# Attention loop on one Trainium2 core: the product with V issued for two loop steps together, at every second step

## What is computed

```python
qkv = x @ qkv_w.T + qkv_b
q, k, v = jnp.split(qkv, 3, axis=2)
scores = jnp.einsum('hbds,hbdt->hbst', q, k) / jnp.sqrt(jnp.float32(hd))
w = jax.nn.softmax(scores, axis=-1)
attn = jnp.einsum('hbst,hbdt->hbsd', w, v)
return attn @ out_w.T + out_b
```

## Time and profile before

| | |
|---|---|
| median of three runs | 601.78 us |
| the profiled execution | 601.03 us |
| its span, first to last instruction | 599.0 us |
| TensorE matmuls busy | 548.1 us (92%) |
| VectorE busy | 479.6 us (80%) |
| ScalarE busy | 349.2 us (58%) |
| L1257, the product with V | 1024 matmuls, 189.5 to 558 us |

### The profile page before, as it was taken

How to read it: one execution, slowest core, us unless ns; L and a number is a source line. 1 busy time by engine, 2 the same in 40 slices (tenths; PEclk the granted TensorE clock), 3 DMA queues, 4 the chain that set the end, 5 groups by cost and what they waited for, 6 DMA issues and landing times.

```text
span 599.0 us, 9634 instructions
## 1 busy us (share of the span) xinstructions
PE 548.1 (92%) x2831; PEld 218.8 (37%) x2831; DVE 479.6 (80%) x965; ACT 349.2 (58%) x667; POOL 112.2 (19%) x155
## 2 busy tenths in 40 slices
PE   2986899885699999999999998999999999999797
PEld 1442567473112333332333332233323333323366
DVE  6999668984598888988888888688888888853573
ACT  2765223245004677777777776677777777778551
POOL 5955906644000001001001000000000000000000
PEclk9997999898555999999999999899999999999999
DMA  8020000013330112001101100200200000000001
GB/s 202 20 52 20 1 1 2 5 48 97 111 113 2 39 43 69 15 1 51 32 2 35 47 2 18 69 2 2 79 2 2 2 2 2 1 2 1 1 19 54
DMA packets 14903, 18.95 MB, mean 32 GB/s; under 512 B 4040, under 2 KB 13175, under 8 KB 13687
## 3 DMA queue, kind: packets, MB, share of 16 engines
q1 hardware_dynamic: 14058, 17.54, 9.8%
q0 software_dynamic: 240, 0.46, 0.7%
q10 hardware_dynamic: 550, 0.27, 0.2%
HBM read 12.75 MB, written 4.19 MB: 28 GB/s over the span
## 4 chain that ended last, share of the span: by engine, by line
PE 73%; DVE 17%; DMA 3%; ACT 3%; issue 2%; SPq 1%; POOL 0%; ACTq 0%; DVEq 0%
PE ps L1257 21%; PE ps L1230 20%; PE ps L1295 18%; PE ps L1035 6%; PE ps L1045 5%; DVE acc L795 3%; DVE mx L896 3%; DVE h L711 2%; DMA k_scr<-gate 1%; DVE acc L841 1%; PE ps L1244 1%; ACT gate L649 1%; DMA kt<-k_scr 1%; DVE st L688 1%; ACT acc L649 1%
## 5 line engine op out<-in xcount | busy, mean ns | idle before, releaser
L896 DVE TENSOR_REDUCE mx<-ps 128x1 f32<-128x512 f32 x512 | 318.8, 681 | 46.6 <-PE ps L1230 41.3
L649 ACT ACTIVATE gate<-ps 128x512 f32<-128x512 f32 x256 | 134.3, 604 | 87.4 <-PE ps L1295 87.4
L1230 PE MATMUL ps<-kt,qt 72*128 72x512 bf16 x384 | 157.7, 417 | 10.6 <-DMA kt<-k_scr 10.6
L649 ACT ACTIVATE acc<-ps 128x512 f32<-128x512 f32 x256 | 132.1, 602 | 49.6 <-PE ps L1295 49.6
L1295 PE MATMUL ps<-qt,kt 96*128 96x512 bf16 x384 | 143.1, 387 | 3.2 <-issue 2.0
L1230 PEld LDWEIGHTS ps<-kt,qt 72*128 72x128 bf16 x384 | 38.3, 100 | 127.0 <-DVE mx L896 83.4
L1257 PE MATMUL ps<-gate,v 128*32 128x512 f32 x512 | 69.1, 611 | 0.7 <-ACT o_sb L640 0.7
L1257 PE MATMUL ps<-acc,v 128*32 128x512 f32 x512 | 69.0, 612 | 0.6 <-ACT acc L649 0.6
L447 POOL CAST nm_s<-nm 16x128 bf16<-16x128 f32 x16 | 4.6, 284 | 305.6 <-DVE nm L909 305.6
L1295 PEld LDWEIGHTS ps<-qt,kt 96*128 96x128 bf16 x384 | 37.4, 99 | 45.5 <-ACT gate L649 6.7
L1230 PE MATMUL ps<-val 72*128 72x512 bf16 x128 | 48.8, 382 | 0.0
(11 more groups left out here) (181 smaller groups left out, 473.7 us busy)
## 6 DMA issues: line engine op xcount, KB each, us to landing
qt<-q_scr SPq DMA_DIRECT2D x18, 192.0 KB
kt<-k_scr SPq DMA_DIRECT2D x18, 192.0 KB
val<-q_scr SPq DMA_DIRECT2D x6, 192.0 KB
val<-k_scr SPq DMA_DIRECT2D x6, 192.0 KB
x<-in_L_attn_a_x SPq DMA_DIRECT2D x4, 256.0 KB, 4.7
us<-h SPq DMA_DIRECT2D x8, 128.0 KB, 2.4
out<-x SPq DMA_DIRECT2D x4, 256.0 KB, 2.2
q_scr<-attn SPq DMA_DIRECT2D x6, 128.0 KB
```

Of the source, the lines that this page charges most:

```text
L649: act.activation(pexp[s % NPB][:, j, :], bank(exp_bank(n0, s * QH + j, last)[0]), ACT.Exp, scale=SCALE).then_inc(exp_done, 1)
L896: dve.tensor_reduce(mx[:, half, u // 2, u % 2:u % 2 + 1], bank(MBANKS[k % 4]), AX.X, ALU.max).then_inc(m_read, 1)
L1230: pe.matmul(bank(MBANKS[k % 4]), qt[r][0:QK_ROWS, half, j, c * P:(c + 1) * P], kt[r][0:QK_ROWS, keys, j, :], start=True, stop=True).then_i ...
```

## The change

```diff
@@ -1295,9 +1295,11 @@
                             j += 1
-                        elif kind == "v" and s:
+                        elif kind == "v" and s % 2 == 0 and s:
+                            pv(r, n, s - 2)
                             pv(r, n, s - 1)
-                        elif kind == "v" and not first:
+                        elif kind == "v" and s == 0 and not first:
+                            pv(prev, n - 1, STEPS - 2)
                             pv(prev, n - 1, STEPS - 1)
@@ -1328,6 +1330,7 @@
             quad(NQ - 1, 0, False, True)
+            pv((NQ - 1) % NBUF, NQ - 1, STEPS - 2)
             pv((NQ - 1) % NBUF, NQ - 1, STEPS - 1)
```

## The result

The changed kernel takes 592.39 us (median of four runs, 591.92 to 593.38), the kernel before 601.44 (600.37 to 601.83) beside it. The ratio is 0.9854 with a 95% interval of 0.9836 to 0.9873: faster by 1.5%, 9.0 us. The forecast was 593.0. The profiled executions stand 9.1 us apart (601.03 and 591.92 us).

What follows compares the result with a forecast made beforehand. TensorE was taken as the bound; 10.4 us saved by pairs + 0.4 at `copy_o` - 0.5 at `turn_o` - 1.5 in quad 7 = 8.8 us, giving 593.0 us (forecast 591 to 595, range 590.5 to 599).

Steps and rivals of the forecast that it cites:

- The bound: Attention loop: TensorE sets the pace, busy the whole window from 192 to 372 us; half a quad takes 23.34 us.
- The junction: Between two adjacent `pv` on TensorE: the second follows like a `pv`'s own second round, 0.455 us, at most 0.63.
- Rivals 1 and 2: Second `pv`'s weight loads exposed, 0.11 us per junction, 599.9 us (chance 0.08); junction costs full turnaround, 0.18 us, 604.3 (0.09).
- The size of a pair: TensorE, two `pv` together: one change in and one out saved, 0.18 us per pair, 10.4 us over 58 pairs.
- The two small terms: First `pv` of a half no longer behind `copy_o`: 0.4 us gained; eighth "m" late at `turn_o`: 0.5 us lost.
- Quad 7: Last quad, no "m" between the "e" from step 4: each pair 0.3 us longer, 1.5 us lost over five.
- The loop's return: Return of the loop: costs 2.4 us once, put down to issue; left out since nothing lengthens the code.
- The room in the banks: Sixteen bf16 matmuls in a row: banks last, with 0.13, 0.09 and 0.04 us to spare; 0.03 late at `turn_o`.
- ScalarE's room: Eighth "e" behind a pair: due at 3.30 us, its bank free at 3.21, 0.09 of room; 0.04 with `copy_o`.

## Why the prediction was right, and where it was right by luck

**The bound** was TensorE, as read: a half quad has four pairs, each 0.23 us shorter in TensorE's rows, and takes 0.92 us less time, with no other engine's work changed.

**The junction**, the unknown of the sum, was taken at 0.455 us, the near end of 0.455 to 0.63. It is 0.43. Rivals 1 and 2 are out: weight loads of the second `pv` are hidden, and no turnaround is paid between two accumulation steps. The Trainium skill's rule on weight loads (TensorE: Matmul & The Clock Gate, The mechanism) doesn't hold in this trace: all strips use all rows, yet the weights of the third round are loaded at 306.05 us under the matmuls of the first `pv`, and the junction is 0.43 us. Its other rule, that only a change of the mode drains the array (TensorEngine Tiling (Array Packing), Key Properties), agrees with both this trace and the kernel with an "m" between.

**The size of a pair** was the first wrong term: 0.18 us forecast, 0.23 measured. I had let all rounds cost 0.455, the one round that the trace of before shows; but that is the first round behind a change of mode, and the later ones are 0.43, two of them per pair. That is 58 x 0.05 = 2.9 us more than the sum said. The two small terms that I had counted apart, 0.4 us gained behind `copy_o` and 0.5 us lost at `turn_o`, are both inside the measured 0.92 us of a half quad.

**Quad 7** was forecast to lose 1.5 us. From step 5's first "e" to step 15's it took 24.10 us (531.03 to 555.13) and takes 24.4 (521.66 to 546.03), 0.3 lost. I had worked out one pair with five banks (4.24 us against 3.94; measured 4.29 and 4.30) and multiplied by five. For the pair with three banks I had forecast 5.20 us against two steps of 2.45; it took 5.28, but the two steps that it replaces had taken 5.18 (531.03 to 536.21), since only the first of them is 2.45 us long. The pairs at steps 10 and 12 stand among `turn_o` and two projections, where TensorE has other work and ScalarE catches up: they gain.

**The loop's return** was left out, "nothing in the change lengthens the code". That was the wrong question. The hole is what remains of the return once the queued matmuls have run, and the change took the last `pv` out from ahead of it. The half quad with the return costs 6.83 us over a plain one, and cost 3.76: 3.1 us lost. The experiment with single `pv` there shows 1.5 of it as the hole. The rest goes with the longer stretch at half level (6.8 us against 3.4), whose cause stays open.

**At the start of the loop** the clock was at half level a little longer than before (0.52 against 0.61 on average in the windows from 182 to 195 us), some 1.2 us of TensorE's time. No step had it. Whether the change does this isn't shown: the two written-out forms of the kernel before have 0.56 and 0.53 in these windows, and every kernel with the change 0.50 to 0.52.

So 8.8 us were forecast and 9.0 measured (9.1 between the profiled executions). In between stand +2.9 for the pairs, +1.2 for quad 7, -3.1 for the return, -1.2 for the clock at the start, and +0.1 for the two small terms; the stretch before the loop adds 0.7 us that the change doesn't explain. These make 9.4, and the last 0.3 us is left open. The mechanism was right, and the direction with it. That the total came within 0.6 us of the forecast was luck: the pairs and quad 7 came out better than the sum had them, by about as much as the return and the start of the loop, which it didn't hold, took away.

**The room in the banks** was right in kind: 0.06 us late per `turn_o` against 0.03 forecast, no hole elsewhere in the sixteen matmuls of a plain half quad. ScalarE's room was smaller than the 0.09 us that I had counted: the last "e" of a stretch starts at 288.32 us and its weights are loaded, behind a wait for ScalarE, at 288.28, which leaves 0.04. With the kernel written out on three engines, 0.06 us more used it up. Groups of three, and `turn_o` one step later, went the way that the counted rooms say, and further.

## What to carry to other kernels

Where two kinds of matmul share the array in different tilings, count the switches: price one from a half period, not from two rows, and group only as far as the banks of the slowest consumer last. Then the order is taut: a piece of work moved by one step can give it all back, as `turn_o` did here. Look at what the moved work used to hide, too, above all where the sequencer must stop.

## What the runs showed of the hardware

- A round of four float32 matmuls in column strips costs 0.43 us when it follows another, and about 0.455 when it is the first behind a change of tiling (305.59 to 306.05). A change costs 0.09 us going in (0.31 against 0.22) and 0.11 coming out (0.54 against 0.43).
- The loop's return stops each engine for 2 to 5 us: TensorE for 2.37 us between matmul starts with a `pv` ahead of it and 4.05 without, ScalarE for 2.63 and VectorE for 2.19 with TensorE written out, VectorE for 4.86 in the kernel before. Writing out one engine's loop leaves the hole with the others; writing out all three removes it.
- Written out on all three engines, ScalarE starts its first exponential behind a pair 0.48 us after the "e", in place of 0.42 with ScalarE's loop.
- The granted clock falls to half level at such a hole, for 3.4 us in the kernel before and 6.7 in the one with single `pv` at the return, with holes of 2.37 and 2.54 us.
